# Self attention of a two-layer gated transformer: the work of a round in another order, the maximum over a shared PSUM bank taken apart, and the weight-folding stage reordered with its row moves kept on chip

## The reference

```python
xn, ln = layernorm(ctx), layernorm(layernorm(x))          # 77 context rows, 1024 latents
q = ln @ W_q
kv = concatenate([xn @ W_kv, ln @ W_kv], axis=1)           # 77 + 1024 = 1101 keys
qn, kn = rmsnorm(q) * SCALE, rmsnorm(k)                    # 4 heads of 64
sim = where(mask, qn @ kn^T, -max); attn = softmax(sim)    # per batch and head 1024 x 1101
out = (attn @ v) @ W_out + b_out
x = x + tanh(g_xattn[0]) * out
```

## Time and profile before

| | |
|---|---|
| median of 3 runs | 1021.39 us (1020.91, 1021.39, 1759.12) |
| profiled execution | 1024.63 us, of it 1022.8 us between the first and the last instruction |
| busy share of that span | PE 83%, PE weight loads 68%, DVE 59%, ACT 36%, POOL 20% |
| mean granted TensorE clock | 0.922 |
| attention rounds, batch 0 and batch 1 | 72.9 to 228.5 and 286.2 to 442.6 us |
| fold | 442.6 to 496.5 us |
| feed-forward, second attention, routing and experts | to 611, 798 and 1022.8 us |

### The profile page before, as it was taken

One profiled execution on the slowest core, in us unless ns is written; L12 is line 12 of the kernel. 1 busy time (PEld: TensorE's weight loads), 2 busy tenths in 40 slices (PEclk: granted clock), 3 DMA queues, 4 the chain that ended last, 5 costly groups with the idle time before them and its releaser, 6 DMA issues.

```text
span 1022.8 us, 14724 instructions
## 1 busy us (share of the span) xinstructions
PE 851.7 (83%) x4566; PEld 692.8 (68%) x4567; DVE 599.7 (59%) x1236; ACT 366.5 (36%) x744; POOL 199.9 (20%) x292
## 2 busy tenths in 40 slices
PE   1866899976759999998899997999999209999996
PEld 0545777754447777763588876888888109999996
DVE  4763777754826777778344437889987502333332
ACT  1433566542525665512433322332332002222221
POOL 4440000001410000020000112445444440111111
PEclk9976999997958999999699998999999658999998
DMA  8400000000000000052400009000000145556540
GB/s 230 81 1 1 1 1 1 1 3 1 1 1 0 2 1 1 1 203 68 146 1 0 1 0 301 29 1 1 1 1 1 55 157 189 179 174 196 158 157 9
DMA packets 46840, 60.13 MB, mean 59 GB/s; under 512 B 16127, under 2 KB 37725, under 8 KB 46653
## 3 DMA queue, kind: packets, MB, share of 16 engines
q1 hardware_dynamic: 30427, 51.93, 15.7%
q0 software_dynamic: 2640, 7.30, 2.0%
q10 hardware_dynamic: 13714, 0.19, 1.0%
HBM read 49.59 MB, written 10.73 MB: 59 GB/s over the span
## 4 chain that ended last, share of the span: by engine, by line
PE 48%; issue 26%; DVE 15%; POOL 5%; ACT 3%; DMA 2%; DVEq 0%; SPq 0%; POOLq 0%; ACTq 0%
PE PS L1673 8%; PE PS L1684 8%; PE PS L965 6%; PE PS L953 5%; PE PS L607 4%; PE PS L1092 3%; PE PS L640 3%; DVE sum L1197 2%; DVE mx L1189 2%; POOL rrms L506 2%; PE PS L1101 2%; PE PS L1110 1%; POOL sorted L1539 1%; PE PS L651 1%; PE PS L652 1%
## 5 line engine op out<-in xcount | busy, mean ns | idle before, releaser
L704 DVE TENSOR_TENSOR PL<-PS,PH 128x512 fp32r<-128x512 f32 x144 | 96.5, 687 | 71.4 <-ACT PH L762 71.0
L762 ACT ACTIVATE PH<-PS 128x512 fp32r<-128x512 f32 x144 | 82.8, 597 | 65.7 <-PE PS L640 63.9
L640 PE MATMUL PS<-ident,prob 128*128 128x128 f32 (+1 forms) x576 | 89.1, 283 | 14.9 <-DVE PL L704 13.6
L640 PEld LDWEIGHTS PS<-ident,prob 128*128 128x128 f32 (+1 forms) x576 | 69.9, 145 | 43.9 <-DVE PL L704 28.1
L607 PE MATMUL PS<-KH,QS 128*128 128x512 f32 (+1 forms) x192 | 79.9, 416 | 22.1 <-ACT prob L755 19.8
L698 DVE TENSOR_REDUCE nmax<-PS 128x1 f32<-128x1101 f32 x64 | 80.5, 1299 | 28.0 <-PE PS L607 27.5
L755 ACT ACTIVATE prob<-PS,nmax 128x1101 f32<-128x1101 f32 x64 | 75.1, 1177 | 49.5 <-DVE nmax L698 49.4
L1673 PEld LDWEIGHTS PS<-xeT,w 128*128 128x128 f32 x736 | 88.4, 197 | 3.7 <-issue 1.4
L1673 PE MATMUL PS<-xeT,w 128*128 128x128 f32 x736 | 88.8, 281 | 2.0 <-ACT xeT L1632 2.0
L1684 PE MATMUL PS<-w,hT 128*128 x368 | 83.1, 379 | 0.0
L1110 PE MATMUL PS<-vw,pcT 128*128 128x256 f32 (+1 forms) x320 | 74.6, 389 | 1.2 <-ACT pcT L1299 1.2
(11 more groups left out here) (248 smaller groups left out, 1565.2 us busy)
## 6 DMA issues: line engine op xcount, KB each, us to landing
w<-in_L_ffn_W SPq DMA_DIRECT2D x31, 1024.0 KB, 5.4
xe<-sorted SPq DMA_DIRECT2D x23, 130.0 KB, 2.1
vw_rows<-vwn SPq DMA_DIRECT2D x2, 1232.0 KB
vw<-vw_rows SPq DMA_DIRECT2D x2, 1152.0 KB, 5.8
XR<-in_x SPq DMA_DIRECT2D x4, 512.0 KB, 7.9
sorted<-fill POOLq DMA_DIRECT2D x1, 1560.0 KB, 11.9
sorted<-fill POOLq DMA_DIRECT2D x1, 1430.0 KB, 8.9
wk<-in_L_xattn_Wk SPq DMA_DIRECT2D x1, 1024.0 KB, 5.7
```

The lines of the kernel that those rows point to most:

```text
L640: last = pe.transpose(PS[0:key_rows(j), bank_of(m, j), s * P:s * P + P], prob[:, m % 2, s, j * P:j * P + key_rows(j)], ident[:])
L704: dve.tensor_tensor(PL[0:r, at, :], PS[0:r, bank_of(m, j), :], PH[0:r, at, :].bitcast(F32), ALU.subtract) \
L762: act.activation(PH[0:r, at, :], PS[0:r, bank_of(m, j), :], ACT.Copy).then_inc(tile_high, 1)
```

## The change

In self attention:

- The maximum of a pair is taken apart. DVE first takes the maximum over the odd tile's 78 columns in the shared bank (`shared_max` into `mshare`), then the even tile's over 1101 as before, and later the odd tile's over the 1023 columns of its own banks (`mown`); a `tensor_tensor` with `ALU.min` (the maxima are negated) joins the two. `exps` now waits for its own maximum and for the shared one, and no longer for the partner's.
- The rounds' calls stand in another order on PE, DVE and ACT, each written as one loop over `m` with calls of rounds that don't exist left out. Scores of a round begin up to two rounds ahead; the two maxima of a pair have a `low_part` or more between them; the two exponentials of a pair have high parts between them. `lsum` gets three buffers.

In the fold:

- PE makes all 16 `kw` products, then all 8 `kc` products, then the 16 value products of batch 0, and no longer these by turns for each pair of heads.
- ACT writes `kwH` and `wfcH`; DVE keeps `kwL` and `wfcL`.
- The values' rows go from `vwn` to `vw` in SBUF directly, in 25 DMAs for each batch (each head's 77 rows, cut where a 128-row chunk ends), counted on four semaphores `vw_moved`. ACT's copies of batch 1 wait for the quarter of batch 0 that they overwrite. The DRAM tensor is gone.

The diff, cut to its core:

```diff
+    OWN_AT = (SHARED + 1) * 512
+    exists_round = lambda m: 0 <= m < MP
+    TURN_ORDER = [(0, 2), (0, 3), (-1, "out 0"), (0, 4), (-1, "out 1"), (0, 5), (0, 6), (0, 7), (0, 8), (1, 0), (1, 1)]
...
+        for m in range(-2, MP + 1):
+            values(m - 1, 8)
+            turn_probs(m, 2)
+            own_scores(m + 1, 3)
+            shared_scores(m + 1, 1)
...
+            own_scores(m + 2, 1)
+            shared_scores(m + 2, 0)
+            turn_probs(m, 7)
+            values(m, 4)
+            turn_probs(m, 8)
+            values(m, 5)
+            values(m, 6)
+            turn_probs(m + 1, 0)
+            values(m, 7)
+            own_scores(m + 2, 2)
+            turn_probs(m + 1, 1)
...
+        def shared_max(m, pair):
+            if exists_round(m):
+                dve.wait_ge(s_done, 2 * (MP * b + m) + pair + 1)
+                dve.tensor_reduce(mshare[:, m % 2, pair:pair + 1], PSf[:, SCORES_AT[1]:OWN_AT], AX.X, ALU.max, negate=True) \
+                   .then_inc(share_ready, 1)
...
+                dve.tensor_reduce(mown[:, m % 2, s // 2:s // 2 + 1], PSf[:, OWN_AT:SCORES_AT[1] + KEYS], AX.X, ALU.max,
+                                  negate=True).then_inc(own_max, 1)
+                dve.wait_ge(own_max, 2 * n + s // 2 + 1)
+                dve.wait_ge(share_ready, 2 * n + s // 2 + 1)
+                dve.tensor_tensor(nmax[:, m % 2, s:s + 1], mown[:, m % 2, s // 2:s // 2 + 1],
+                                  mshare[:, m % 2, s // 2:s // 2 + 1], ALU.min).then_inc(max_ready, 1)
...
-            act.wait_ge(max_ready, GT * (MP * b + m) + s - s % 2 + 2)
+            if m >= 2 and s == 0:
+                act.wait_ge(t_done, KT * (MP * b + m - 1))
+            act.wait_ge(max_ready, GT * (MP * b + m) + s + 1)
+            act.wait_ge(share_ready, 2 * (MP * b + m) + s // 2 + 1)
...
+            if b > 0 and h % 4 == 0:
+                act.wait_ge(vw_moved[h // 4], 16 * b * len(pieces_of(h // 4)))
...
-                own.add(dve.tensor_copy(kwH[:, k, :, cols], product))
-                own.wait()
-                bank.read(dve.tensor_tensor(kwL[:, k, :, cols], product, kwH[:, k, :, cols].bitcast(F32), ALU.subtract))
+            dve.wait_ge(kw_high, i + 1)
+            bank.read(dve.tensor_tensor(kwL[:, k, :, cols], product, kwH[:, k, :, cols].bitcast(F32), ALU.subtract))
...
-            rows = t["vw_rows"][b]
-            sp.dma_start(rows.rearrange("(h c) n -> c h n", c=C), vwn[:]).then_inc(vw_out[b], 16)
-            sp.wait_ge(vw_out[b], 16)
-            whole = HK // P
-            sp.dma_start(vw[:, b, 0:whole, :], rows[0:whole * P, :].rearrange("(t p) n -> p t n", p=P)).then_inc(vw_in, 16)
-            sp.dma_start(vw[0:HK - whole * P, b, whole, :], rows[whole * P:HK, :]).then_inc(vw_in, 16)
+            for quarter in range(4):
+                for h, c0, c1, chunk, row in pieces_of(quarter):
+                    if c0 == 0:
+                        sp.wait_ge(vwo_read, H1 * b + h + 1)
+                    sp.dma_start(vw[row:row + c1 - c0, b, chunk, :], vwn[c0:c1, h, :]).then_inc(vw_moved[quarter], 16)
```

More of the change, by code:

```diff
@@ L343, in layers_kernel @@
     x_in = [sem(f"x_in{k}") for k in range(NG)]
-    vw_out = [sem(f"vw_out{k}") for k in range(B)]
+    vw_moved = [sem(f"vw_moved{k}") for k in range(4)]
     xe_in = [sem(f"xe_in{k}") for k in range(4)]
@@ L573, in layers_kernel @@
     SHARED = 2
[L575 to L579 removed]
+    OWN_AT = (SHARED + 1) * 512
+    exists_round = lambda m: 0 <= m < MP
+    TURN_ORDER = [(0, 2), (0, 3), (-1, "out 0"), (0, 4), (-1, "out 1"), (0, 5), (0, 6), (0, 7), (0, 8), (1, 0), (1, 1)]
+    TURNS = [(m + o, x) for m in range(-2, MP + 2) for o, x in TURN_ORDER if exists_round(m + o)]
     bank_of = lambda m, x: 5 + TURNS.index((m, x)) % 2
@@ L614, in own_scores @@
         def own_scores(m, s):
-            scores(m, s, False)
+            if exists_round(m):
+                scores(m, s, False)
         def shared_scores(m, pair):
+            if not exists_round(m):
+                return
             if GT * m + 2 * pair >= 2:
@@ L652, in values @@
             pe.matmul(PS[:, 7, :], v, PL[0:r, at, :], start=False, stop=j == KT - 1).then_inc(pv_done, 1)
-        for pair in range(2):
-            own_scores(0, 2 * pair)
-            own_scores(0, 2 * pair + 1)
-            shared_scores(0, pair)
-        for m in range(MP):
-            own = (lambda s: own_scores(m + 1, s)) if m + 1 < MP else (lambda s: None)
-            shared = (lambda pair: shared_scores(m + 1, pair)) if m + 1 < MP else (lambda pair: None)
-            out = (lambda half: project_out(m - 1, half)) if m > 0 else (lambda half: None)
-            own(0)
-            turn_probs(m, 0)
-            turn_probs(m, 1)
-            own(1)
-            shared(0)
-            if m > 0:
-                values(m - 1, 7)
-                values(m - 1, 8)
+        for m in range(-2, MP + 1):
+            values(m - 1, 8)
@@ L904, in dve_fold @@
         ffn_norm(dve, 0)
-        for k in range(KC):
-            for c4 in range(0, FC, 4):
-                k0 = bank.to_read()
-                high, low = (w[:, k, c4 * P:c4 * P + 4 * P] for w in (wfcH, wfcL))
-                own.add(dve.tensor_copy(high, PS[:, k0, :]))
-                own.wait()
-                bank.read(dve.tensor_tensor(low, PS[:, k0, :], high.bitcast(F32), ALU.subtract))
+        for i in range(KC * 2):
+            k, c4 = i // 2, i % 2 * 4
+            k0 = bank.to_read()
+            high, low = (w[:, k, c4 * P:c4 * P + 4 * P] for w in (wfcH, wfcL))
+            dve.wait_ge(wfc_high, i + 1)
+            bank.read(dve.tensor_tensor(low, PS[:, k0, :], high.bitcast(F32), ALU.subtract))
         for c2 in range(0, FC, 2):
@@ L916, in layers_kernel, with pieces_of @@
     FOLD_BANKS, VWO_BANKS = [0, 1, 2, 3, 4], [5, 6, 7]
-    FOLD_ALL = 1 + FC // 2 + 2 * FC + 3 * FC + FC
+    FOLD_KW = 1 + FC // 2 + 2 * FC
+    FOLD_WFC = FOLD_KW + 3 * FC
+    FOLD_ALL = FOLD_WFC + FC
+    def pieces_of(quarter):
+        pieces = []
+        for h in range(4 * quarter, 4 * quarter + 4):
+            at = h * C
+            while at < h * C + C:
+                end = min(h * C + C, at - at % P + P)
+                pieces.append((h, at - h * C, end - h * C, at // P, at % P))
+                at = end
+        return pieces
+    VW_PIECES = sum(len(pieces_of(q)) for q in range(4))
     def sp_fold(sp):
@@ L1148, in pe_cross @@
         pe.wait_ge(lif_done, 2 * NG + 2)
-        pe.wait_ge(vw_in, 16 * 2 * B)
+        for quarter in range(4):
+            pe.wait_ge(vw_moved[quarter], 16 * B * len(pieces_of(quarter)))
         pe.wait_ge(cross_in, 16 * CROSS_LOADS)
```

187 lines of the change are left out of this document (101 added, 86 removed).

## The result

The changed kernel takes **996.9 us** (median of 4 runs, 995.9 to 998.0) where the kernel before takes 1021.2: a ratio of 0.9761, 95% interval 0.9745 to 0.9776. It is faster by 24 us; the forecast was 993. One of the kernel before's four runs took 1759.12 us, and the ratio leaves it out. The profiled execution takes 997.27 us with a span of 995.5.

What follows compares the result with a forecast made beforehand. PE was taken as nearest to the bound in attention, DVE then the rows' landing in the fold. Attention 20.3 plus fold 8 wins 28.3 us: profiled 1024.6 becomes 996, median 993, range 982 to 1006.

Steps and rivals of the forecast that it cites:

- The steady round: Attention: one pipelined round falls from 16.82 to 15.2 us, ends 14.9 and 15.8.
- The three gaps: Attention: PE stands still 1.25 us behind the output's second half, 0.44 before block 0, about 0.2 before the last block.
- The rival of a loosened tie: Attention: engine crossings cost 0.2 us more, rounds take 15.9, attention wins only 12 us, time 1001; 19 in 100.
- PE's own work is 14.9 us a round: Attention: PE's 16.82 us round less its idle places; no order can beat that.
- two chains that tie: Attention, round's end: DVE's chain of 4.3 us and ACT's, within 0.1, against PE's work of 4.2.
- The first blocks 2.4 us later: Attention, each batch's start: one more step of maximum and exponential, less overlap, delays the first blocks 2.4 us (1 to 4).
- seven rounds in 105.2: Attention: first to last block 2 of a batch, six rounds of 15.2, a seventh of 13.5, plus 0.5 for the clock.
- Normalization 5.0 to 5.3 us earlier: Fold: 16 products at PE's pace (9.1), eight `kc` pairs at DVE's (7.9), 0.4 hand-over: 17.4 us instead of 22.4.
- 25 DMAs at about 0.45 us of SP's time: Fold: issue time of each row move; with 2.1 us to land, the last quarter arrives at 483.1.
- the early quarters land before ACT wants them: Fold: ACT waits only for the fourth quarter of moved value rows, under 2 us.
- the moves gate the fold: Fold: few DMA engines share a piece, last quarter lands at 489, 3.5 to 5.5 us won, time 996; 12 in 100.
- one after another: Fold: each piece holds the next until landed, 52.5 us, fold ends at 524, time 1029; 3 in 100.

Runs made afterwards that it cites:

- attn_two: Changed kernel's attention with the earlier kernel's fold (high parts on DVE, moves through device memory), plus two value-row buffers: 999.5 us, 0.9782 of the kernel before.
- two_buffers: Changed kernel with the second batch's value rows in a buffer of their own: 987.4 us, 0.9661 of the kernel before.
- rows16: Changed kernel with all 25 pieces a batch cut to 32, 48 or 64 rows, same bytes in all: 991.2 us, 0.9695 of the kernel before.
- dram_moves: Changed kernel with the value rows moved through device memory again, as in the kernel before: 998.2 us, 0.9760 of the kernel before.

## Why the prediction was right or wrong, point by point

The total was right to 4 us, but partly by luck: its errors partly cancel. For the profiled execution it said 1024.6 - 28.3 = 996.3, and 997.3 came: the attention won 2.6 us more than its term, the fold 4.3 less, the rest of the program 0.7 on its own. The other 2.9 us of the 3.9 is the step from the profiled execution to the median: I took 3.2 off, as in the kernel before; the changed kernel's profiled execution stands only 0.4 above its median.

- *The steady round: right.* 15.2 forecast, 15.2 measured, in both batches. The small reduction costs 0.24 us with a slot of 0.16 (347.14 to 347.30), the odd maximum 1.21, the join 0.16 with a slot of 0.10. DVE is busy for 12.93 us of the round (13.1). The three gaps closed. The rival of a loosened tie, 15.9 us a round, did not come.
- *"PE's own work is 14.9 us a round", and 0.3 of waits at two chains that tie: not refuted.* PE counts as busy for all of the 15.20 us, but that count hides short waits: in the kernel before it leaves only 1.2 us idle of 16.85, where the starts show gaps of 1.9. The loads of weights still wait three times, once ahead of block 0, where the forecast looked for it. How much of the 15.20 is work and how much wait, no run separates.
- *The first blocks 2.4 us later, seven rounds in 105.2: right.* Block 2 came at about 98.6, 2.4 later, and 104.2 us lie between (in batch 1 too). Batch 0 won 10.4 up to its last block 2 (9.4 forecast), and 12.5 of the 22.9 came behind that (10.9 forecast).
- *Why the order wins: half seen.* I priced the maximum's separation as a cost of 0.5 us a round and the new order as the gain. The runs show that the order without it loses 1.7 us a round against the kernel before: the separation is what lets the order work.
- *Normalization 5.0 to 5.3 us earlier, at 30.5 behind the fold's start: right* (30.1, 5.7 earlier). What it would bring was read wrongly: the fold before was taken to wait for the rows' landing, where `attn_two` shows DVE's `wfcL` behind the normalization. The products took 8.7 us (9.1), the `kc` pairs 8.0 (7.9). The first row move started at 26.8 behind the fold's start (27.1).
- *"25 DMAs at about 0.45 us of SP's time": the step that failed.* They took 0.78. The first starts on time and the last quarter is waited for until 48.2 us behind the fold's start, where I had 40.5: 7.7 later, and 24 x 0.33 = 7.9. With it fell "the early quarters land before ACT wants them", the wait under 2 us (8.7) and the full clock at the fold's end. I had a row of 0.59 us for a move in hand and went below it. Without the waits (`two_buffers`) the fold is 10.5 us shorter than before, more than the 8 forecast, so the rest of the term was not what failed.
- *The rival "the moves gate the fold": its outcome, not its reason.* It said 996 and 3.5 to 5.5 us won in the fold; 996.9 and 3.7 came. But it had the rows of the busiest engine as the limit, and no quarter waited for such an engine: it was complete 2.1 to 2.7 us after its last piece's issue began. The limit is the queue that issues them. Its threshold of 0.6 us a piece is not contradicted: at 0.64 ACT still waits for 3.6 us.
- *The rival "one after another": excluded*, as it needs 1.6 us a piece.
- *What I didn't ask:* whether the moves need to be waited for at all. The reuse of one buffer held back more of this stage (6.9 us) than the change won in it (3.7).

## What to carry to other kernels

Two edits that serve the same round have to be priced together: here the separation alone gives 0.4%, the order alone costs over 2.5%, and both give 2.2%. Where TensorE stood still for 4 us, the lower clock behind the wait cost as much again: the next three groups of the fold took 4.3 us more. A transfer that somebody waits for only because its source is written again is best cured by another buffer, not by a faster transfer; 50 pieces and 6 instructions were then equally fast. Where rows must be moved in pieces, count the pieces times the queue's time for one, taken at least from the slowest row at hand (0.59 us here, and 0.78 came), cut them to multiples of 16 rows where the layout allows it, and don't issue them from an engine that is itself waited for.

## What the runs showed of the hardware

- The length of a DMA issue on SyncE's queue changes with the piece and does not grow with its bytes: 24 rows of 1 KB take 0.78 us from start to start, 53 rows 0.67, 77 rows 0.81 to 0.89, and 32, 48 or 64 rows 0.64 alike (`rows16`). On ACT's queue a piece takes about 0.8 us.
- A quarter's small SBUF to SBUF transfers were complete 1.9 to 2.7 us after the last one's issue began, without a backlog.
- The granted clock fell to 0.50 after PE had stood still for 4 to 4.5 us (`attn_two`, 456.5 to 460.5; `dram_moves`, 455 to 459), and stayed there for the rest of the fold although PE was then busy for 10.7 of 11 us (`dram_moves`, 461 to 472).
- Four transposes and eight value products took 3.71 us at a granted clock of 0.50 and 2.3 us at 1.00.
